# Gated delta rule, triangular inverse: levels four and five as 64x64 diagonal blocks, with a new order of work in a turn

## The reference

```python
decay = where(tril, exp(g[..., :, None] - g[..., None, :]), 0)
M = where(stril, einsum('bhncd,bhnmd->bhncm', k_beta, k) * decay, 0)
T = solve_triangular(eye + M, eye, lower=True)     # inverse of a unit lower triangle
v_c = einsum('bhnij,bhnjd->bhnid', T, v_beta)
...
out_i = (q_i * exp(g_i)) @ state + (q_i @ k_i.T * dec_i) @ v_new
h = norm_w * rmsnorm(out) * silu(z)
out = einsum('bsf,df->bsd', h, W_out)
```

## Time and profile before

| | us |
|---|---|
| median of 3 runs | 952.99 |
| lowest, highest | 947.33, 955.03 |
| the profiled execution | 946.55 |
| its span | 944.8 |
| mean granted clock of PE | 0.897 |

### The profile page before, as it was taken

One profiled execution on the slowest core, in us unless ns is written; L12 is line 12 of the kernel. 1 busy time (PEld: TensorE's weight loads), 2 busy tenths in 40 slices (PEclk: granted clock), 3 DMA queues, 4 the chain that ended last, 5 costly groups with the idle time before them and its releaser, 6 DMA issues. The chain is left out here.

```text
span 944.8 us, 13981 instructions
## 1 busy us (share of the span) xinstructions
PE 785.4 (83%) x5047; PEld 618.3 (65%) x5048; DVE 503.0 (53%) x1202; ACT 386.9 (41%) x999; POOL 193.7 (21%) x376
## 2 busy tenths in 40 slices
PE   5756459999999998982269999999999959995997
PEld 4655348988988887861136676676676837783654
DVE  1615817856768654326426556566666225453561
ACT  1505756545444544432315555555555312222220
POOL 1014875154555446000000000000000000000000
PEclk9657769989999999975659999999999979997899
DMA  5005111722222211100098111111110051000000
GB/s 219 1 1 224 28 31 44 272 71 73 66 63 63 57 40 40 32 9 0 0 241 192 19 26 31 25 32 23 34 24 7 12 217 52 1 1 0 1 1 11
DMA packets 49123, 53.95 MB, mean 57 GB/s; under 512 B 33856, under 2 KB 38976, under 8 KB 47808
## 3 DMA queue, kind: packets, MB, share of 16 engines
q1 hardware_dynamic: 47776, 50.95, 17.9%
q0 software_dynamic: 1280, 2.12, 2.2%
HBM read 51.69 MB, written 1.36 MB: 56 GB/s over the span
## 5 line engine op out<-in xcount | busy, mean ns | idle before, releaser
L1527 ACT COPY d_Pt<-bank 128x512 f32<-128x512 f32 x96 | 51.6, 589 | 101.6 <-PE bank L1450 101.6
L1602 DVE TENSOR_REDUCE d_nm<-scores 128x1 f32<-128x1024 f32 x64 | 75.4, 1219 | 20.4 <-PE scores L1443 20.4
L1004 DVE SCALAR_TENSOR_TENSOR b_yc<-b_cpad,b_slab,b_yc 128x256 f32<-128x256 f32 x192 | 80.0, 487 | 0.0
L1539 ACT ACTIVATE d_Pr<-scores,d_negm 128x1024 f32<-128x1024 f32 x64 | 70.8, 1111 | 17.7 <-DVE d_negm L1605 17.7
L1450 PEld LDWEIGHTS bank<-cst,d_Pr 128*128 128x128 f32 x512 | 56.2, 141 | 29.4 <-issue 24.7
L1450 PE MATMUL bank<-cst,d_Pr 128*128 128x128 f32 x512 | 69.2, 278 | 0.7 <-DVE d_Pt L1579 0.4
L1443 PE MATMUL scores<-d_KM,d_Q 64*128 64x512 f32 x256 | 65.4, 630 | 2.0 <-ACT d_Q L1518 2.0
L1463 PE MATMUL bank<-d_Pt,d_KV 128*64 128x128 f32 x1024 | 63.0, 276 | 0.0
L645 PE MATMUL bank<-xnT,b_slab 128*128 128x256 f32 x256 | 60.1, 389 | 2.5 <-ACT b_cpad L866 2.5
L1463 PEld LDWEIGHTS bank<-d_Pt,d_KV 128*64 128x64 f32 x1024 | 55.2, 137 | 7.8 <-issue 5.8
L645 PEld LDWEIGHTS bank<-xnT,b_slab 128*128 128x128 f32 x256 | 49.1, 197 | 9.5 <-issue 3.1
(11 more groups left out here) (326 smaller groups left out, 1713.0 us busy)
## 6 DMA issues: line engine op xcount, KB each, us to landing
b_slab<-in_b_slab SPq DMA_DIRECT2D x16, 520.0 KB, 3.6
b_wz<-in_b_wz SPq DMA_DIRECT2D x16, 256.0 KB, 2.9
b_wo<-in_b_wo SPq DMA_DIRECT2D x16, 256.0 KB, 2.9
d_w<-in_d_w SPq DMA_DIRECT2D x16, 224.0 KB, 2.5
b_DT<-b_cs SPq DMA_DIRECT2D x2, 1536.0 KB, 10.2
f_w<-in_f_w SPq DMA_DIRECT2D x3, 896.0 KB, 10.9
c_w<-in_c_w SPq DMA_DIRECT2D x2, 1024.0 KB, 7.7
d_wo<-in_d_wo SPq DMA_DIRECT2D x1, 2048.0 KB, 7.9
```

Of the source, the lines that this page charges most:

```text
L1004: last = dve.scalar_tensor_tensor(yc[x][:, ch], src, tap, yc[x][:, ch], ALU.mult, ALU.add)
L1527: act.copy(Pt[g][:].rearrange("p j q -> p (j q)"), TP[g % 2]).then_inc(pt_cp[g % 2], 1)
L1539: act.activation(Pr[b][:, keys], scores[:, 2 * k:2 * k + 2, :].rearrange("p g k -> p (g k)"), ACT.Exp, bias=negm[:, b:b + 1], accum_out=su ...
L1602: last = dve.tensor_reduce(nm2[:, b, k:k + 1], scores[:, 2 * k:2 * k + 2, :].rearrange("p g k -> p (g k)"), AX, ALU.max, negate=True)
```

## The change

Levels 0 and 1 (four and five of seven) work only on the two 64x64 diagonal blocks. `T` is kept as 64 columns for each problem instead of 128: rows 0-63 hold the upper block, rows 64-127 the lower. `level_y` and `level_z` issue for each problem one matmul for rows and output partitions 0-63 and one for 64-127 (`DIAG`), instead of one of 128x128. `level_turn` transposes rows 0-63 by `transpose` and rows 64-127 by a matmul against the identity. The copies take 128x256 instead of 128x512; the masks are 64 wide, and only the two used remain in the constants. The transpose has a tile of its own (`Tt`) for levels 0 and 1; for the last level it goes into `TT` by two copies, and TT's remaining quarter is set to zero once at the stage's start. `sz` is doubled.

PE's and ScalarE's order in a turn is new, as below: gate 0 goes ahead of level_y 0, project 1 is split around level_z 0, y_out goes behind level 1's y and turn, gate 1 behind level_z 1, and squares 1 and key product 1 ahead of level_z 2. On DVE conv 1 is whole, and keys take x = 1 first. On SyncE blocks_back goes behind next_slab(j, 1) and next_wz(i, 1); on GpSimd rotate_latents (turns 2 to 5, work for a later stage) goes ahead of solve.

```diff
-C_LVT = C_LV + LEVELS * P
-C_CQ = C_LVT + LEVELS * P
+C_CQ = C_LV + P
 C_SQ = C_CQ + 2 * TOK
...
     HALF = P // 2
+    DIAG = (slice(0, HALF), slice(HALF, P))
...
+    Np, T, Vh = two("Np", [P, 2, U, P]), two("T", [P, 2, U, HALF]), two("Vh", [P, 2, U, P])
     G, S, tmp = (sb(n, [PROBLEMS, W, W]) for n in ("G", "S", "tmp"))
-    TT, Ys, vn, sz, hs, hT = (two(n, [P, U, P]) for n in ("TT", "Ys", "vn", "sz", "hs", "hT"))
+    TT, vn, hs, hT = (two(n, [P, U, P]) for n in ("TT", "vn", "hs", "hT"))
+    sz = [two(f"sz{k}", [P, U, P]) for k in range(2)]
+    Tt, Ys = two("Tt", [P, U, HALF]), two("Ys", [P, U, HALF])
     carrier = sb("carrier", [P, 2 * LEV])
     m8, r8 = sb("m8", [P, 2, 2, B]), sb("r8", [P, 2, 2, B])
...
-        m = cst[:, C_LV + level * P:C_LV + (level + 1) * P].bitcast(U32)
-        return m.unsqueeze(1).to_broadcast([P, U, P])
+    def half(ap):
+        return ap[:, 0:U * HALF].rearrange("p (u k) -> p u k", u=U)
+
+    def mask(k):
+        m = cst[:, C_LV + k * HALF:C_LV + (k + 1) * HALF].bitcast(U32)
+        return m.unsqueeze(1).to_broadcast([P, U, HALF])
 
     def has(i):
...
                 for k in range(NB):
                     at = slice(k * W, (k + 1) * W)
-                    sp.dma_start(T[j % 2][at, :, :, at].rearrange("p x u c -> p (x u) c"), solved[k].rearrange("u c n -> c u n")).then_inc(t_in, 16)
+                    to = slice(k * W % HALF, k * W % HALF + W)
+                    sp.dma_start(T[j % 2][at, :, :, to].rearrange("p x u c -> p (x u) c"), solved[k].rearrange("u c n -> c u n")).then_inc(t_in, 16)
...
                 if i >= 1:
                     next_wo(i)
+                if has(j + 1):
+                    next_slab(j, 1)
+                if i >= 0 and has(i + 1):
+                    next_wz(i, 1)
                 if has(i + 1):
                     blocks_back(i + 1)
-                if i >= 0 and has(i + 1):
-                    next_wz(i, 1)
-                if has(j + 1):
-                    next_slab(j, 1)
...
         def _(pool):
             for x in range(2):
                 pool.memset(cpad[x][:], 0.0).then_inc(pads_set, 1)
+                pool.memset(TT[x][:], 0.0).then_inc(pads_set, 1)
             env["ln_gpsimd"](1)
             pool.wait_ge(s["cst_in"], 16)
...
                     power(i - 1)
                 if has(i + 1):
                     clear(i + 1)
+                if 1 < i < 6:
+                    env["w_d"]["rotate_latents"](i - 2)
+                if has(i + 1):
                     solve(i + 1)
                 if i == -1:
                     for j in range(5, PAIRS):
                         hide(j)
                 if has(i + 2):
                     norm(i + 2)
-                if 1 < i < 6:
-                    env["w_d"]["rotate_latents"](i - 2)
             power(PAIRS - 1)
...
                 for u in range(U):
+                    to = slice(u * HALF, (u + 1) * HALF)
                     if not last_level:
-                        last = pe.matmul(YZ[x][:, u * P:(u + 1) * P], n[:, x, u, :], t[:, x, u, :], start=True, stop=True)
+                        for q in DIAG:
+                            last = pe.matmul(YZ[x][q, to], n[q, x, u, q], t[q, x, u, :], start=True, stop=True)
                     else:
-                        last = pe.matmul(YZ[x][HALF:, u * P:u * P + HALF], n[:HALF, x, u, HALF:], t[:HALF, x, u, :HALF],
+                        last = pe.matmul(YZ[x][HALF:, to], n[:HALF, x, u, HALF:], t[:HALF, x, u, :],
                                          start=True, stop=True)
                 last.then_inc(y_mm, 1)
...
                 for u in range(U):
-                    last = pe.transpose(ZT[x][:, u * P:(u + 1) * P], T[i % 2][:, x, u, :], ident)
+                    to = slice(u * HALF, (u + 1) * HALF)
+                    pe.transpose(ZT[x][:HALF, to], T[i % 2][:HALF, x, u, :], ident[:HALF, :HALF])
+                    last = pe.matmul(ZT[x][HALF:, to], T[i % 2][HALF:, x, u, :], ident[HALF:, HALF:], start=True, stop=True)
                 last.then_inc(tr_mm, 1)
...
                 for u in range(U):
+                    to = slice(u * HALF, (u + 1) * HALF)
                     if k < LEV - 1:
-                        last = pe.matmul(YZ[x][:, u * P:(u + 1) * P], TT[x][:, u, :], Ys[x][:, u, :], start=True, stop=True)
+                        for q in DIAG:
+                            last = pe.matmul(YZ[x][q, to], Tt[x][q, u, :], Ys[x][q, u, :], start=True, stop=True)
                     else:
-                        last = pe.matmul(YZ[x][:HALF, u * P + HALF:(u + 1) * P], Ys[x][HALF:, u, :HALF], TT[x][HALF:, u, HALF:],
+                        last = pe.matmul(YZ[x][:HALF, to], Ys[x][HALF:, u, :], TT[x][HALF:, u, HALF:],
                                          start=True, stop=True)
                 last.then_inc(zz_mm if k < LEV - 1 else zt_mm, 1)
...
             def apply(i, x):
+                pe.wait_ge(pads_set, 4)
...
             for i in TURNS:
                 j = i + 2
                 front, value, solving, behind = has(j), has(i + 1), has(i), has(i - 1)
-                if solving:
-                    level_y(i, 0, 0)
-                    level_y(i, 0, 1)
                 if front:
                     project(j, 0)
                 if i == -2:
                     sums()
                 if solving:
                     gate(i, 0)
-                for x in range(2):
-                    if behind:
-                        turn_h(i - 1, x)
+                    level_y(i, 0, 0)
+                    level_y(i, 0, 1)
+                if front:
+                    project(j, 1, range(0, 2))
+                if behind:
+                    turn_h(i - 1, 0)
+                    turn_h(i - 1, 1)
                 if solving:
                     level_turn(i, 0, 0)
                     level_turn(i, 0, 1)
-                if front:
-                    project(j, 1)
                 if value:
                     values(i + 1, 0)
                 if solving:
                     level_z(i, 0, 0)
                     level_z(i, 0, 1)
+                if front:
+                    project(j, 1, range(2, 4))
                 if value:
                     values(i + 1, 1)
-                if behind:
-                    y_out(i - 1)
                 if solving:
                     for x in range(2):
                         level_y(i, 1, x)
                         level_turn(i, 1, x)
-                    gate(i, 1)
+                if behind:
+                    y_out(i - 1)
+                if solving:
                     level_z(i, 1, 0)
                     level_z(i, 1, 1)
                 if front:
                     squares(j, 0)
                 if solving:
+                    gate(i, 1)
                     for x in range(2):
                         level_turn(i, 2, x)
                         level_y(i, 2, x)
+                if front:
+                    squares(j, 1)
+                    key_products(j, 1)
+                if solving:
                     level_z(i, 2, 0)
                     level_z(i, 2, 1)
-                if front:
-                    squares(j, 1)
-                if solving:
                     apply(i, 0)
                     apply(i, 1)
                 if front:
                     key_products(j, 0)
-                    key_products(j, 1)
                 if solving:
                     attend(i, 0)
                     attend(i, 1)
...
-                act.activation(sz[x][:].rearrange("p u k -> p (u k)"), PZ, ACT.Silu).then_inc(sz_done, 1)
+                act.activation(sz[i % 2][x][:].rearrange("p u k -> p (u k)"), PZ, ACT.Silu).then_inc(sz_done, 1)
...
                 if k < LEV - 1:
-                    act.copy(Ys[x][:], quad(YZ[x])).then_inc(y_cp, 1)
+                    act.copy(Ys[x][:], half(YZ[x])).then_inc(y_cp, 1)
                 else:
-                    act.copy(Ys[x][HALF:, :, :HALF], quad(YZ[x])[HALF:, :, :HALF]).then_inc(y_cp, 1)
+                    act.copy(Ys[x][HALF:], half(YZ[x])[HALF:]).then_inc(y_cp, 1)
 
             def level_turn(i, k, x):
                 act.wait_ge(tr_mm, 2 * LEV * i + 2 * k + x + 1)
-                act.copy(TT[x][:], quad(ZT[x])).then_inc(tt_cp, 1)
-
-            act.wait_ge(pads_set, 2)
+                if k < LEV - 1:
+                    act.copy(Tt[x][:], half(ZT[x])).then_inc(tt_cp, 1)
+                else:
+                    act.copy(TT[x][HALF:, :, HALF:], half(ZT[x])[HALF:])
+                    act.copy(TT[x][:HALF, :, :HALF], half(ZT[x])[:HALF]).then_inc(tt_cp, 1)
+
+            act.wait_ge(pads_set, 4)
             for i in TURNS:
                 j = i + 2
                 front, value, solving, behind = has(j), has(i + 1), has(i), has(i - 1)
                 for x in range(2):
                     if behind:
                         outputs(i - 1, x)
-                if solving:
-                    level_y(i, 0, 0)
-                    level_y(i, 0, 1)
                 if front:
```

(39 more changed lines are left out.)

4 lines of the change are left out of this document (1 added, 3 removed).

## The result

| | before | after |
|---|---|---|
| median, us | 950.16 (4 runs) | 1003.09 (4 runs) |
| lowest, highest | 946.93, 955.03 | 1002.30, 1006.93 |
| the profiled execution | 946.55 | 1002.61 |
| its span | 944.8 | 1000.8 |
| mean granted clock of PE | 0.897 | 0.872 |

The change makes the kernel slower: ratio 1.0561, 95% interval 1.0499 to 1.0622. Of the 56 us of span, 54 come up to the end of the stage that the diff touches. Turns are measured here from one gate(i, 0) to the next, since the head of a turn has moved: gate(0, 0) starts at 141.62 (before 141.24), gate(6, 0) at 399.99 (361.08), the first matmul of the next stage at 487.88 (433.89). Six turns brought 38.5 us, turns 6 and 7 15.1, the start 0.4, the rest of the program 2.0.

A forecast was written before the change was run, and what follows sets the result against it. PE's own queue was taken as the bound. Six turns x 6.3 = 38, turns 6 and 7 14, start 1, clock 5: +58 on 946.6 gives 1005, as median 1006 us; own range 980 to 1035, overall 928 to 1032.

The forecast's parts named there:

- The bound: In the stage the diff touches, PE's own queue sets the time; PE busy 36.36 of 37.84 us in a full turn.
- The alternation of transpose and matmul: In level_turn, each switch between quadrant transpose and 64x64 matmul is a change of shape costing 0.145 us; 60 changes a turn.
- the 1.8 named as the sign: In PE's timeline, a level_turn call's 12 instructions take about 1.8 us if changes are paid, 0.5 to 0.7 if not.
- The sum of the levels: A turn's levels on PE go from 12.2 to 18.5 us with 60 changes of shape: +6.3 us a turn.
- Clock: PE's granted clock: up to two more slow stretches in each of the first six turns, 0 to 20 us, taken as 5.
- Waits: PE's waits in a turn: Ys of the last level -1.15, apply +0.15, gate(i, 0) +1.0; sum 0.
- The new wait before gate(i, 0): PE waits at gate(i, 0) for DVE's chain, 0.8 to 1.6 us a turn, taken as 1.0.
- Start: At the stage's start, two memsets of TT on GpSimd ahead of the layer norm's POW add 1.0 us once.
- Turns 6 and 7: The last two solving turns add 2 x 6.3, plus level_y (1.8) no longer under gate's wait in turn 6: 14 us.
- Rival 1: In level_turn the transpose shares the quadrants' shape: 14 changes, -1.8 us a turn, about 935 us; chance 0.27 with overlap, 0.07 without.
- Rival 2: Diagonal quadrants writing one bank don't overlap: eight level_y and level_z calls double, +30 us, 1036 with alternation; chance 1 in 5.
- Rival 3: The new order stalls on at_done more than reckoned: 1 us a turn is +8, inside the ranges; no separate chance.

The follow-up runs named there:

- the grouped kernel: The changed kernel with level_turn issuing its four transposes first and its four matmuls after, two groups a call instead of eight: 943.9 us, ratio 0.9935 against the kernel before.

## Why the prediction was right

The forecast was 1006 us, slower; 1003.1 came. The direction and its cause hold: the alternation is paid, and taking it out alone turns 5.6% slower into 2.6% faster. By the prediction's own steps:

- **The bound.** Right: PE's queue sets the time; PE is busy 44.03 of 44.37 us in a full turn, and the time went where PE's instructions went.
- **The alternation of transpose and matmul.** Right in kind, over-sized. A problem takes 0.43 us where the sum had 3 x 0.058 + 2 x 0.145 = 0.465, a call 1.72 us against the 1.8 named as the sign. The price of one change is 0.13 (from the grouped kernel), not 0.145, a price taken from full-width neighbours.
- **The sum of the levels.** Right in kind, 1.3 us a turn too large. From start to start, at the full clock, a turn's levels take 1.08 + 8 x 0.43 + 1.08 + 4.51 + 1.08 + 4.14 + 1.23 = 16.6 us, in the order of the queue. The z of level 0 and of level 2 ran at the low clock here; 1.08 is that of level 1, and 1.23 is from the kernel with both halves by matmul. PE's timeline of the kernel after, turn 2:

```profile
239.88 0.68 PE L743 MATMUL scores<-b_T,b_Np 64*64 64x64 f32 x16
...
244.39 3.72 PE L725 MATMUL bank<-b_wo,b_hT 128*128 128x256 f32 x16
248.04 1.15 PE L769 MATMUL scores<-b_Ys,b_Tt 64*64 64x64 f32 x32
249.12 0.66 PE L665 MATMUL bank<-cst,b_qkv 128*128 128x128 f32 x4
...
251.44 0.24 PE L757 MATMUL scores<-cst,b_T 64*64 64x64 f32 x1
...
255.58 0.75 PE L665 MATMUL bank<-cst,b_qkv 128*128 128x128 f32 x4
256.12 1.92 PE L677 MATMUL bank<-b_qkv 128*128 128x256 f32 x4
257.97 1.79 PE L771 MATMUL scores<-b_TT,b_Ys 64*64 64x64 f32 x16
259.69 2.05 PE L780 MATMUL scores<-b_Vh,b_TT 128*128 128x128 f32 x16
```

  That isn't all that the islands cost. The full-width groups that border on them are longer than the same groups in the run with full levels in the same order: gate 0 by 0.10 us, half of project 1 by 0.10, values 1 by 0.09, `y_out` by 0.20 (3.65 against 3.45), squares 0 by 0.06, gate 1 by 0.10, together 0.65; attend, which borders on none, takes 1.79 in both. So part of the price of a change falls on the neighbour, and the levels cost 16.6 + 0.65 - 12.2 = +5.0 us a turn, not +6.3. For the islands of y and z the forecast was near: 1.08 us and 0.2 at the neighbours against 0.93 + 0.29. Too large were the price of an alternation, and levels 1 and 2, where PE overlaps the end of `level_turn` with the `level_y` that follows on another quadrant.
- **Clock.** The step that failed. The prediction named the stretch at the low clock as a result of long islands of short groups, and took 5 us for all turns. The groups that ran at the low clock in turn 2 took 0.36 + 0.45 + 0.82 + 1.36 + 0.89 + 0.49 = 4.4 us more than the same groups at the high one (end of `level_turn`, values, z, project, key product, z of level 2; the high one read here or in the kernel with both halves by matmul), against 1.7 in one turn before: +2.7 a turn, some 16 us if all six turns were like it (an estimate). The prediction had 0 to 20 us for it and a mechanism, but took the low end without a reason: 5 us is one more slow stretch in every second turn, where by its own sum every turn has three islands of 17 or 18 short groups.
- **The errors cancel.** Per turn +5.0 + 2.7 - 1.15 = +6.6, measured 44.37 - 37.84 = +6.5, forecast 6.3 for the levels, 0.8 for the clock and nothing for the waits. Levels and waits were 1.3 and 1.15 us too high, the clock 1.9 too low. The total came out within 3 us (+58 us forecast, +56 measured on the profiled executions) in part by luck: the number deserves less trust than its distance suggests.
- **Waits.** `Ys` of the last level: gone, as forecast, -1.15. The new wait before gate(i, 0), forecast 1.0: absent in full turns, 2.5 us before gate(6, 0) where it had been 1.46. The length of DVE's chain was read from the end of turn 5, and norm's part of it was drawn out there by GpSimd, as in every turn with `rotate_latents`. DVE's timeline of the kernel before, and then of the kernel after:

```profile
241.32 0.62 DVE L1015 TENSOR_TENSOR b_r<-b_r 128x4 f32<-128x4 f32 x1
...
242.18 1.12 DVE L1018 SCALAR_TENSOR_TENSOR b_vi<-b_m,b_r 128x4 f32<-128x4 f32 x1
...
243.41 1.23 DVE L1021 SCALAR_TENSOR_TENSOR b_rq<-b_rqs 128x4 f32<-128x4 f32 x1
244.68 0.61 DVE L1032 SCALAR_TENSOR_TENSOR b_Np<-bank,b_nb,b_DT 128x128 f32<-128x128 f32 x2
```

```profile
262.39 0.15 DVE L1038 TENSOR_TENSOR b_r<-b_r 128x4 f32<-128x4 f32 x1
...
262.78 0.16 DVE L1041 SCALAR_TENSOR_TENSOR b_vi<-b_m,b_r 128x4 f32<-128x4 f32 x1
...
263.05 0.16 DVE L1044 SCALAR_TENSOR_TENSOR b_rq<-b_rqs 128x4 f32<-128x4 f32 x1
263.25 0.87 DVE L1055 SCALAR_TENSOR_TENSOR b_Np<-bank,b_nb,b_DT 128x128 f32<-128x128 f32 x3
```

From the first norm operation to the first of `keys` 3.4 us (244.68 - 241.32) became 0.9. In turn 5 before, from which the chain of the earlier trace rows comes, it was 2.6 us (354.97 to 357.60). The prediction costed the move of `rotate_latents` at nothing; the run with it put back, where PE waits 1.7 us, shows that the move is what keeps the wait away.
- **Start.** +1.0 forecast, +0.4 measured. Turns 6 and 7: 14 forecast, 15.1 measured, the share of the clock in it larger.
- **Rivals.** Rival 1 (transpose shares the quadrants' shape) is false: 0.43 us a problem, not 0.12. Rival 2 (no overlap in one bank) is false as well: 32 instructions in 1.08 us, and slower when issued quadrant by quadrant. Gotcha 1 of the Trainium skill's "TensorEngine Tiling (Array Packing)", by which different row tiles can't use one PSUM bank at once, gave that rival; the measurement decides against it for diagonal quadrants that write different partitions. Rival 3: no stall at `at_done` in full turns.

Left open: whether a transpose and a matmul can't follow each other closely for a difference of width or of mode; both explanations fit every run here.

## What to carry to other kernels

Cutting matmuls to the blocks that aren't zero paid here only once all groups side by side in an island were of one kind: a transpose of a quadrant that alternates with 64x64 matmuls cost 0.13 us at each border, and writing it as a matmul with the identity, one more instruction, took 79 us off. Count the borders between kinds in the new queue before counting columns, and look at the granted clock behind each long stretch of them: here two of three were followed by the low level. When work for later moves on GpSimd, look at which small operations of DVE lie beside its old and its new place, not only at who waits for it.

## What the runs showed of the hardware

- **Quadrants.** Matmuls of 64x64 on the two diagonal quadrants, into one PSUM bank, run side by side: 32 in 1.08 us, 0.034 us an instruction with the changes at both ends, against 0.058 alone (the kernel after).
- **Alternation.** An fp32 transpose of a quadrant and the fp32 64x64 matmul beside it: 0.43 us a problem in turns, 0.24 in groups of four (0.94 us a call).
- **Clock.** 2.4 GHz, granted clock 1.00, in turns 1 to 5 of the kernel with both halves by matmul, of the one with transposes and matmuls apart, and of the one with full levels in the new order; 0.88 to 0.92 in those of the kernel after, 0.91 to 0.96 where level 0 alone alternates. PE is shown as busy all the time in the alternating stretches. At the low clock a group of 64-wide tiles went from 1.08 to 1.90 us and one of 256 columns from 1.83 to 3.19.
- **DVE and GpSimd.** Operations of DVE on 128x4 and 128x8 between SBUF tiles take 0.16 us alone; beside a `tensor_tensor` of GpSimd the rows shown have 0.6 to 1.25 us, the end falling within 0.03 us of GpSimd's, and beside a back-to-back chain of twelve one took 8.16 us. Beside a memset of GpSimd it stayed at 0.16.
